# One more border in the tile order of a mixture-of-experts kernel, with earlier loads and reordered last steps for batches 4 and 5

## What is computed

```python
def reference(emb, W_Q, W_K, W_V, gate_w, gate_b, w1, b1, w2, b2, ln_g, ln_b):   # emb: 8 x 512 x 128, float32
    x = layernorm(emb + causal_attention(emb @ W_Q, emb @ W_K, emb @ W_V))
    logits = (x @ gate_w + gate_b) / 0.9                 # 8 experts
    gate_probs = softmax over the two largest logits
    h = gelu(x @ w1[e] + b1[e])                          # 128 -> 512, for each chosen expert
    y = sum over the two experts of gate_probs * (h @ w2[e] + b2[e])
    return layernorm(x + layernorm(y) * ln_g + ln_b)
```

## Time and profile before

| | us |
|---|---|
| median of three runs | 259.19 (258.05 to 260.06) |
| the profiled execution's own time | 257.17 |
| its span, first to last instruction | 255.4 |
| PE busy | 229.6 (90%) |
| ACT busy | 179.3 (70%) |
| DVE busy | 173.4 (68%) |
| POOL busy | 144.3 (57%) |
| part of PE in the chain that ended last | 78% of the span |

### The profile page before, as it was taken

How to read it: one execution, slowest core, us unless ns; L and a number is a source line. 1 busy time by engine, 2 the same in 40 slices (tenths; PEclk the granted TensorE clock), 3 DMA queues, 4 the chain that set the end, 5 groups by cost and what they waited for, 6 DMA issues and landing times.

```text
span 255.4 us, 7300 instructions
## 1 busy us (share of the span) xinstructions
PE 229.6 (90%) x1874; PEld 209.0 (82%) x1875; DVE 173.4 (68%) x958; ACT 179.3 (70%) x527; POOL 144.3 (57%) x165
## 2 busy tenths in 40 slices
PE   6988998999999799999999999999999999999100
PEld 3466876788787689999999999999999999999100
DVE  0146576787888888558953333366488999989884
ACT  3365857778675889977886555555555996599953
POOL 8400007357777777777877777775544545546500
PEclk9999999999999999999999999999999999999855
DMA  5999303023131545523328797868789686913275
GB/s 143 250 332 332 105 3 93 31 74 97 53 95 53 137 134 120 144 68 107 95 75 254 204 355 241 221 183 246 228 267 356 186 232 180 320 47 114 92 220 151
DMA packets 45105, 42.38 MB, mean 166 GB/s; under 512 B 5488, under 2 KB 34080, under 8 KB 45072
## 3 DMA queue, kind: packets, MB, share of 16 engines
q1 hardware_dynamic: 40224, 32.84, 45.2%
q0 software_dynamic: 4320, 8.92, 10.0%
q10 hardware_dynamic: 528, 0.26, 0.3%
HBM read 27.89 MB, written 12.01 MB: 156 GB/s over the span
## 4 chain that ended last, share of the span: by engine, by line
PE 78%; DVE 10%; ACT 5%; DVEq 2%; issue 2%; DMA 1%; ACTq 0%; SPq 0%
PE bank L595 26%; PE bank L584 25%; PE bank L435 6%; PE bank L462 4%; PE bank L502 3%; PE bank L421 3%; PE bank L483 2%; ACT rows L668 2%; PE bank L450 2%; ACT probs L676 2%; PE bank L426 2%; PE bank L592 2%; PE bank L416 1%; DMA wk<-in_L_attn_W_K_dram 1%; DVE sum_stats L1139 1%
## 5 line engine op out<-in xcount | busy, mean ns | idle before, releaser
L749 ACT ACTIVATE h<-bank,b_cols 128x128 f32<-128x128 f32 x284 | 81.6, 385 | 37.4 <-PE bank L584 37.0
L1340 POOL DMA_INDIRECT returned<-x,slot_back x71 | 71.3, 1004 | 43.0 <-DVE x L1120 33.2
L1335 POOL DMA_INDIRECT slots<-rows,slot_of x64 | 65.0, 1016 | 53.0 <-DVE rows L984 34.4
L595 PE MATMUL bank<-w_all,h 128*128 x568 | 78.5, 282 | 0.0
L584 PE MATMUL bank<-slot_xT,w_now 128*128 128x128 f32 x568 | 75.2, 275 | 0.1
L595 PEld LDWEIGHTS bank<-w_all,h 128*128 128x128 f32 x568 | 69.0, 192 | 0.8
L584 PEld LDWEIGHTS bank<-slot_xT,w_now 128*128 128x128 f32 x568 | 69.1, 192 | 0.3 <-DVE slot_xT L883 0.3
L881 DVE CAST slot_back<-slot_x 128x1 uint32<-128x1 f32 x71 | 10.4, 147 | 37.9 <-PE bank L584 37.8
L838 DVE TENSOR_REDUCE negmax<-bank 128x1 f32<-128x128 f32 (+3 forms) x32 | 14.7, 484 | 16.0 <-PE bank L436 15.8
L462 PEld LDWEIGHTS bank<-v,probsT 128*128 128x128 f32 x160 | 19.7, 192 | 5.7 <-issue 3.8
L1120 DVE TENSOR_SCALAR x<-bank,slot_gate 128x128 f32<-128x128 f32 x71 | 24.0, 341 | 0.2 <-PE bank L595 0.2
(11 more groups left out here) (155 smaller groups left out, 305.4 us busy)
## 6 DMA issues: line engine op xcount, KB each, us to landing
w_now<-in_L_ffn_w_dram SPq DMA_DIRECT2D x47, 256.0 KB, 3.6
slot_x<-slots SPq DMA_DIRECT2D x71, 65.0 KB
w_all<-in_L_ffn_w_dram SPq DMA_DIRECT2D x16, 256.0 KB, 5.9
pair<-returned SPq DMA_DIRECT2D x14, 256.0 KB, 3.2
rows<-rows SPq DMA_DIRECT2D x8, 256.0 KB, 3.0
x<-n_L_attn_embeddings_dram SPq DMA_DIRECT2D x7, 256.0 KB, 3.9
returned<-x,slot_back POOLq DMA_INDIRECT x71, 3.4
slots<-rows,slot_of POOLq DMA_INDIRECT x64, 2.3
```

The lines of the kernel that those rows point to most:

```text
L595: m = nc.tensor.matmul(o, h[:, s % RING, c * P:(c + 1) * P], w2_c, start=False, stop=(c == FC - 1))
L749: m = nc.scalar.activation(h[:, s % RING, cols], bank_[:, cols], ACT.Gelu, bias=b1_cols[:, c:][:, bass.ds(first, 1)])
L1335: g_.indirect_dma_start(slots, bass.IndirectOffsetOnAxis(ap=slot_of[:, b, c:c + 1], axis=0), rows[:, k, b * TB + t, :], None).then_inc(dis ...
L1340: g_.indirect_dma_start(returned, bass.IndirectOffsetOnAxis(ap=slot_back[:, j:j + 1], axis=0), y[:, j % Y_RING, :], None).then_inc(y_retur ...
```

## The change

PARTS gets a border behind batch 4, at 47 tiles. `passed` and the other rows of the second table grow with NP from 5 to 6, and batch 4's route copies its count into `totals`. Batch 4's pair loads stand behind tile 61 in SyncE's order instead of 69, with a wait for the returns of 47 tiles; batch 5's stand behind tile 69 instead of 70, with the wait for 55 tiles that stood ahead of batch 4's. In FINAL batch 4's first steps go between batch 2's and batch 3's, and batch 4's centring goes ahead of batch 5's first steps. The sum of the costs stays 148, and the code behind the list is the same.

```diff
--- before.py
+++ after.py
@@ -43,7 +43,7 @@
 
 
     HALF = TB // 2
-    PARTS = (4 * 2, 6 * 2, 7 * 2, 7 * 2 + 1, 8 * 2)
+    PARTS = (4 * 2, 5 * 2, 6 * 2, 7 * 2, 7 * 2 + 1, 8 * 2)
     NP = len(PARTS)
     REGION = N + P
     SLOTS = REGION * E + (E - 1) * P
@@ -243,7 +243,7 @@
             return [16 * len(range(s, end, Y_RING)) for s in range(Y_RING)]
 
 
-        LOAD_AT = {b: WHOLE[0] + 15 + b for b in range(4)} | {b: WHOLE[1] + 10 + b for b in (4, 5)}
+        LOAD_AT = {b: WHOLE[0] + 15 + b for b in range(4)} | {b: WHOLE[b - 3] + 14 for b in (4, 5)}
         LN_B_AT = WHOLE[0] - 3
         FINAL_AT, FINAL_SHARE = WHOLE[0] + 7, 6
         NORM_FROM, NORM_AT, OUT_AT, ROOT_AT = 2 * TB, 55, 67, (52, 65)
@@ -379,8 +379,8 @@
                         load_w1(j - W1_LAG, experts[j - W1_LAG - first_w1])
                     for b, at_j in LOAD_AT.items():
                         if isinstance(i, int) and j == at_j:
-                            if b in (0, FIRST):
-                                wait_whole(0 if b < FIRST else 1)
+                            if b == 0 or b >= FIRST:
+                                wait_whole(max(b - 3, 0))
                             load_pair(b)
 
             for i in range(1, BOUND):
@@ -390,11 +390,11 @@
                 body(i)
             for k, e in enumerate(tile_experts(J - W1_LAG, W1_LAG)):
                 load_w1(J - W1_LAG + k, e)
-            wait_whole(2)
+            wait_whole(3)
             load_pair(B - 2)
-            wait_whole(3)
+            wait_whole(4)
             load_pair(B - 1)
-            wait_whole(4)
+            wait_whole(5)
             load_pair(B)
 
             out_p = out.rearrange("b (t p) d -> p (b t) d", p=P)
@@ -1181,9 +1181,10 @@
             FINAL = [(what, b, cost) for b in range(4) for what, cost in HEAD]
             FINAL += [("centre", 0, 5), ("centre", 1, 5), ("root", 0, 3)]
             FINAL += [(what, b, cost) for b in (0, 1) for what, cost in FUSED[1:]]
-            FINAL += [(what, b, cost) for b in (2, 3) for what, cost in PLAIN]
-            FINAL += [(what, b, cost) for b in (4, 5) for what, cost in HEAD]
-            FINAL += [("centre", 4, 5), ("centre", 5, 5), ("root", 1, 3)]
+            FINAL += [(what, 2, cost) for what, cost in PLAIN]
+            FINAL += [(what, 4, cost) for what, cost in HEAD]
+            FINAL += [(what, 3, cost) for what, cost in PLAIN]
+            FINAL += [("centre", 4, 5)] + [(what, 5, cost) for what, cost in HEAD] + [("centre", 5, 5), ("root", 1, 3)]
             FINAL += [(what, b, cost) for b in (4, 5) for what, cost in FUSED[1:]]
 
             def finished_by(j):
```

## The result

| | median, us | lowest to highest, us | ratio to before, 95% interval |
|---|---|---|---|
| before (20 runs) | 258.68 | 257.04 to 260.39 | |
| changed (20 runs) | 260.76 | 259.60 to 262.56 | 1.0092 (1.0068 to 1.0115) |
| changed, a second set (4 runs; before 258.48) | 261.26 | 260.92 to 261.98 | 1.0122 (1.0091 to 1.0152) |

The change costs 2.4 us by the ratio (1.8 to 3.0 by the interval; the medians differ by 2.1): within 1%, on the slow side. The forecast was 260.6 us. One of the twenty changed runs took 308.04 us, at a granted clock of 0.74 where the others had 0.96 to 0.97; it stands in the median, and in neither the range nor the ratio.

What follows compares the result with a forecast made beforehand. PE's unbroken row of tiles and, behind it, DVE's tail were taken to set the end. The larger table's 0.65 us plus the last steps' order's 0.75 gave 1.4 us on a 259.19 us median: 260.6 us, range 258.3 to 262.0.

Steps and rivals of the forecast that it cites:

- The larger table: DVE's three passes over `passed` grow 1.15 us, tile 24's slot load goes out late, PE stops: +0.65 us.
- row of moved bytes: DMA moved 130 KB from 131.50 to 132.10 us, so tile 24's load landed no sooner than 1.6 us after issue.
- The order of DVE's last steps: Batch 5's aggregate moves behind centre 4, so ACT's second root and then the fourth root's reciprocal are late: +0.75 us.
- the aggregate's place: Batch 5's aggregate on DVE goes from tile 64 to tile 65, ending at 226.75 us; second root waits 0.75 us.
- The extra copy: Copy of `totals` in batch 4's route on DVE, short and ahead of spare time: 0.
- The loads that come sooner: Pair loads of batches 4 and 5 issued earlier by SyncE; the profiled execution waits for neither: gain 0.
- the rival of the pair loads: DVE's pair loads were late in ordinary runs; 2.0 us of waiting removed gives 258.6 us; chance 0.07.
- SyncE's new wait: At tile 61 SyncE waits for tile 46's return; tile 62's slot load goes to about 199.1 us: cost 0.
- Hidden terms: Rival: both lateness terms, tile 24's load and ACT's second root, are hidden: +0, 259.2 us; chance 0.25.
- Slow load of slot 24: Rival: tile 24's moved load takes 4.2 us, sharing queues with GpSimd's return; PE stops 2.9 us, 262.9 us; chance 0.10.
- Tile 25: Rival: tile 25's slot load, behind GpSimd's last dispatch, sets PE's stall: up to 0.3 us more, 260.9 us; chance 0.08.
- The rule that stood beside tile 25: DVE instructions with two SBUF inputs contend with GpSimd instructions reading SBUF, reductions do not; sum 1.4 to 1.7 us.

Runs made afterwards that it cites:

- the border alone: The kernel before with only the sixth border, behind batch 4, loads and last steps at their old tiles: 259.71 us, ratio 1.0068.
- the two borders: The kernel before with two more borders, behind batch 4 and in the middle of batch 5, loads and order as before: 261.07 us, ratio 1.0102.
- the load taken ahead of the table: The changed kernel with SyncE issuing tile 24's row load ahead of its wait for the expert numbers: 259.93 us, ratio 1.0069.
- centre first: The kernel before, five borders, with only batch 4's centring moved ahead of batch 5's first steps: 258.43 us, ratio 1.0007.
- the order undone: The changed kernel with the old order of DVE's last steps put back, border and sooner loads kept: 259.86 us, ratio 1.0079.
- one copy more: The kernel before with one more DVE copy of 8 elements in batch 4's route, into a tile nobody reads: 259.45 us, ratio 1.0047.
- second run: The kernel before with only the sixth border, behind batch 4, unaltered and run again: 260.30 us, ratio 1.0084.
- first try: The kernel before with only the sixth border, where by a slip the last three pair loads waited for the very last border: 268.94 us, ratio 1.0418.

## Why the prediction was right, and where it was not

The time, 260.6 against 260.76 us, hides two errors that cancel in part. The base was too high: 259.19 us was the median of three runs, that of twenty is 258.68. And the sum was too small: 1.4 us against 2.1 by the medians and 2.4 by the ratio. That the two nearly meet is luck.

**The larger table: the right place, the term too small.** The passes take 2.45 us (2.44 by the forecast's working), and `expert_of` starts 2.02 us later than in before, of which PE's delay up to there is 0.85: 1.17 for the table, where the forecast had 1.15. Two steps behind it were mis-sized. The write of `expert_of` itself takes 0.39 us, where it took 0.17, so the load goes out 0.2 us later than forecast. It takes 0.38 to 0.40 us in all ten profiles with six borders and 0.17 in the four with five or seven; why is open. Its row in DVE's timeline:

```profile
130.96 0.39 DVE L999 TENSOR_SCALAR expert_of<-found 1x46 int32<-1x46 int32 x1
```

The other is the landing. Between its bounds of 1.6 and 2.42 us the forecast took about 1.9, nearer to the row of moved bytes. For before that reading was right: the trace has the load's last part in 1.79 us after its issue, at 132.27 us, and the windows view shows no bytes behind it:

```profile
132.10:132.70 0.60, 0.60 (x8) 0.60 (x7) 0.00 (x0) 0.60 (x3) 0.29 (x2) 1.00 0.00 0
```

But it doesn't carry over to the moved load, which lands in 1.94 and 2.09 us in the changed kernel's two profiles, 2.33 and 2.31 with the border alone, and 1.9 to 2.5 over the nine profiles in which it stands behind a longer table. With the border alone 0.65 + 0.2 + (2.33 - 1.92) = 1.26 us, and 1.25 is what PE waited; in the changed kernel it was 1.02. What sets the landing within that spread is open. That it is the table's length is shown by the two borders (more of it) and by the load taken ahead of the table (none of it, and no wait).

**The order of DVE's last steps: the mechanism was right, the term too small.** The second root waits, gelus are late behind it, and the fourth root's reciprocal waits 0.50 us. But the root waits 1.40 us instead of 0.75 (1.11 in the first profile), which is more than the 0.68 us of room ahead of contract(70), and in the profile all of it reaches the end: PE is 2.03 us late from tile 25's transpose (136.93 us against 134.90) to tile 70's and 2.88 at contract(70), so it loses 0.85, forecast at 0.1 at most, and DVE's reciprocal loses another 0.55. The step that failed is the aggregate's place: 228.99 us is 4.41 later than in before, of which PE's delay is 2.0 and the forecast's step 1.79. The remaining 0.6 us are DVE's waits for the pairs of batches 0 to 3, which the forecast left out. The view of DVE's waits, before, centre first, changed:

```profile
DVE pair L1135 <- DMA pair<-returned: 0.4, 1, 0.4
```

```profile
DVE pair L1135 <- DMA pair<-returned: 0.5, 1, 0.5
```

```profile
DVE pair L1135 <- DMA pair<-returned: 1.3, 3, 0.7
```

How they reach the root is in DVE's timeline: the additions of pairs of batch 3 in before, then of batches 2, 3 and 5 in the changed kernel (batch 5's of before is in the earlier trace rows):

```profile
195.94 0.69 DVE L1135 TENSOR_TENSOR pair<-pair 128x512 f32<-128x512 f32 x1
```

```profile
195.75 0.69 DVE L1135 TENSOR_TENSOR pair<-pair 128x512 f32<-128x512 f32 x1 [0.66 <-DMA pair<-returned]
...
198.51 0.69 DVE L1135 TENSOR_TENSOR pair<-pair 128x512 f32<-128x512 f32 x1
...
226.67 0.69 DVE L1135 TENSOR_TENSOR pair<-pair 128x512 f32<-128x512 f32 x1
```

From batch 3's to batch 5's DVE takes 26.33 us in before and 28.16 in the changed kernel. It is 28.1 to 28.2 us in all six profiles with centre 4 ahead and, waits for batch 5's own load set aside, 26.3 to 26.4 in the eight others. So DVE's list has no spare time there, and a wait for an earlier batch reaches the root whole. Of the six, the two with 0.3 and 0.5 us of such waits have 0.47 and 0.55 at the root, the four with 1.0 to 1.4 have 1.11 to 1.40; with the order undone 2.4 us of them make the root wait 0.39 without the move. No run changed these waits alone. By the times the order is worth 0.2 us alone and 0.35 undone, with intervals that hold 0 and 1.

**The extra copy: forecast at 0, and that was wrong.** "Short and ahead of spare time" holds for its own duration. What was not thought of is that it moves the whole instruction stream by one place. One consequence, as far as the table of packets shows, is tile 6's wait (0.59 and 0.75 us in the two profiles). Another stands in DVE's tail, where nothing covers it: a pause that no semaphore ends (`issue`). The timelines of DVE, one line each: before with 958 instructions, changed with 959, two borders with 960:

```profile
249.19 0.69 DVE L1166 SCALAR_TENSOR_TENSOR pair<-pair,sum_moments,lng 128x128 f32<-128x128 f32 x2
```

```profile
252.94 0.61 DVE L1166 SCALAR_TENSOR_TENSOR pair<-pair,sum_moments,lng 128x128 f32<-128x128 f32 x2 [0.23 <-issue]
```

```profile
254.37 0.16 DVE L1128 SCALAR_TENSOR_TENSOR sum_shift<-sum_moments,sum_rstd 128x2 f32<-128x2 f32 x1 [0.43 <-issue]
```

In all nine profiles with 959 instructions 0.23 us stand ahead of this line, in the four with 958 none, and with 960 the pause is one instruction earlier and longer. That is the last 0.2 us of the table of places. Together the copy's two effects make 0.8 us in the profiled execution. Alone, it had 1.2 us by the times (0.5 to 2.0) and 0.1 by the profile, so what it costs an ordinary execution is not shown.

**The loads that come sooner: 0, as forecast.** No wait of DVE for batch 4's or 5's pairs is in the changed kernel's profiles. With the old loads batch 5's was late in three of seven profiles: by 0.25 us (one copy more), 0.27 (border alone, second run) and 0.93 (its first try). That is the rival of the pair loads; it exists, at less than half of the 2.0 us that it had in the forecast.

**SyncE's new wait: 0, as forecast,** though tile 62's slot load went out at 202.67 us and not at 199.1.

**The rivals.** Hidden terms: ruled out by the waits. Slow load of slot 24: it didn't happen there (1.9 to 2.5 us, where the rival needed 3.1), but the same thing, a load of 3.7 us, happened at tile 6, where the forecast didn't look. Tile 25: it appears only once tile 24's wait is taken away, 0.17 and 0.12 us.

The rule that stood beside tile 25 in the forecast (the Trainium skill, SBUF — State Buffer, "Who interferes with whom") is borne out by GpSimd's timeline. An indirect DMA of 0.96 us takes 3.15 and 3.21 us beside the two passes with two SBUF inputs, and 0.95 beside the reduction:

```profile
120.92 3.15 POOL L1336 DMA_INDIRECT slots<-rows,slot_of  x1 [0.30 <-issue]
124.37 3.21 POOL L1336 DMA_INDIRECT slots<-rows,slot_of  x1 [0.30 <-issue]
127.89 0.95 POOL L1336 DMA_INDIRECT slots<-rows,slot_of  x1 [0.30 <-issue]
```

## What to carry to other kernels

Where PE runs without a gap for 100 us, ask of every added instruction, however short, which transfers are within a microsecond of being late: here two loads and one root were, and each turned a delay of about a microsecond into the whole kernel's. A load's landing is not one number: here the same load took 1.8 us before and 1.9 to 2.5 after, so where the consumer's margin is smaller than that spread, carry the spread into the sum. And a wait that appears where the edit changes nothing can come from a packet of instructions beside a load, and its place differs between executions of one program: repeat the profile before giving such a wait a price.

## What the hardware showed that was not expected

A packet of 16 KB of instructions shares the DMA engines with the data: it holds one of them for 1.4 us (1.0 to 1.8 over nine traces), and a slot load of 65 KB that goes out 0.3 to 0.9 us ahead of it lands in 3.2 to 4.1 us instead of 2.1 to 2.4, for one of its sixteen parts. The Trainium skill (Runtime: NRT & Kernel Launch, "Instruction fetch mechanics") says that an engine's instructions come in 16 KiB blocks, fetched ahead by its own queue, at a cost that is mostly hidden. The size agrees with the trace; the cost is not hidden here from the load beside it. Whether DVE's own pauses of 0.23 and 0.43 us belong to such blocks no run shows.

The times of one kernel spread over more than 3 us, and part of that is PE's clock at the start: full clock begins at 7.6 to 9.4 us in ten traces and at 13.3 to 13.5 us in four, which take tile 5's operand 2.0 to 2.3 us later than the one of before. Where a set holds more of these, its median rises whatever the edit. The copy of 8 elements alone, 0.47% (0.18 to 0.77) over before by its times and 0.1 us by its profile, may be such a case; that is open.
